# Two changes to a cross-attention loop: where max rows are turned, and which engine reads 8 of 52 max units

## The reference

```python
q = (x @ Wq + bq).reshape(Bq, Tq, 16, 8)        # 1024 queries
k = (ctx @ Wk + bk).reshape(Bk, Tk, 16, 8)      # 6404 keys
v = (ctx @ Wv + bv).reshape(Bk, Tk, 16, 8)
scores = einsum('bqhd,bkhd->bhqk', q, k) / sqrt(8)
attn = softmax(scores, axis=-1)
out = einsum('bhqk,bkhd->bqhd', attn, v).reshape(...) @ wo + bo
```

## Time and profile before

| | us |
|---|---|
| median of 3 runs | 4839.96 (4836.34 to 4844.47) |
| the profiled execution | 4841.48 |
| its span, first to last instruction | 4839.6 |
| busy PE / DVE / ACT / POOL in it | 3934.6 / 3448.6 / 2863.0 / 258.7 |
| busy DVE in max units (L1510) | 2801.6 |
| busy ACT in exponentials (L1497) | 2471.6 |
| mean granted TensorE clock | 0.853 of full |

### The profile page before, as it was taken

The page is one execution under the profiler, slowest core; times in us unless marked ns, Lnnn a source line. Parts: engine busy times, 40 slices in busy tenths (PEclk is TensorE's granted clock), DMA queues, the critical chain, the costliest instruction groups (busy, mean ns, idle before and its releaser), DMA issues. The chain is left out here.

```text
span 4839.6 us, 83868 instructions
## 1 busy us (share of the span) xinstructions
PE 3934.6 (81%) x34310; PEld 1295.2 (27%) x34310; DVE 3448.6 (71%) x3258; ACT 2863.0 (59%) x4073; POOL 258.7 (5%) x183
## 2 busy tenths in 40 slices
PE   6897478988898855888988898479747988898885
PEld 2563222222222212222222222135422222222221
DVE  4332488888888615888888885389848888888871
ACT  1332157777777741677777777335414777777774
POOL 3000000000000010000000000234310000000000
PEclk9556579999998985899999989789957999999998
DMA  2000310111111012110111010100041111011100
GB/s 83 1 0 11 70 22 13 24 24 24 16 21 24 4 37 59 23 24 13 23 24 24 13 24 4 43 19 5 3 81 16 19 24 24 14 23 24 24 2 20
DMA packets 103596, 114.10 MB, mean 24 GB/s; under 512 B 58672, under 2 KB 93712, under 8 KB 98256
## 3 DMA queue, kind: packets, MB, share of 16 engines
q1 hardware_dynamic: 103248, 109.19, 13.3%
HBM read 83.56 MB, written 25.60 MB: 23 GB/s over the span
## 5 line engine op out<-in xcount | busy, mean ns | idle before, releaser
L1510 DVE TENSOR_REDUCE chunk_max<-max_scores 128x2 f32<-128x1024 f32 (+1 forms) x2496 | 2801.6, 1179 | 534.5 <-PE max_scores L1399 408.3
L1497 ACT ACTIVATE probs<-scores 128x512 f32<-128x512 f32 (+1 forms) x3231 | 2471.6, 809 | 907.8 <-PE scores L1425 751.9
L1425 PE MATMUL scores<-queries,key_ring 49*128 49x512 bf16 x4800 | 1288.4, 404 | 244.0 <-ACT probs L1497 129.5
L1452 PE MATMUL values_sum<-probs,values 128*9 128x256 f32 x19584 | 1446.6, 402 | 1.7 <-ACT probs L1497 1.7
L1399 PE MATMUL max_scores<-key_ring,queries 48*128 48x512 bf16 (+1 forms) x4992 | 979.0, 411 | 216.1 <-DVE chunk_max L1510 154.2
L1452 PEld LDWEIGHTS values_sum<-probs,values 128*9 128x9 f32 x19584 | 386.8, 91 | 893.6 <-issue 626.1
L1425 PEld LDWEIGHTS scores<-queries,key_ring 49*128 49x128 bf16 x4800 | 313.1, 95 | 1141.7 <-ACT probs L1497 877.6
L1399 PEld LDWEIGHTS max_scores<-key_ring,queries 48*128 48x128 bf16 x4992 | 249.7, 97 | 645.7 <-DVE chunk_max L1510 555.9
L1057 ACT ACTIVATE probs<-scores 128x512 f32<-128x512 f32 x256 | 138.5, 592 | 106.1 <-PE scores L1009 106.1
L1524 DVE COPY values_sum_s<-values_sum 128x256 f32<-128x256 f32 x48 | 20.1, 418 | 235.0 <-PE values_sum L1452 235.0
L1083 DVE TENSOR_REDUCE chunk_max<-max_scores 128x1024 f32 (+1 forms) x128 | 154.9, 1213 | 23.6 <-PE max_scores L965 23.4
(11 more groups left out here) (176 smaller groups left out, 1944.1 us busy)
## 6 DMA issues: line engine op xcount, KB each, us to landing
key_ring<-k_parts SPq DMA_DIRECT2D x96, 300.2 KB
key_ring<-k_parts SPq DMA_DIRECT2D x96, 200.1 KB
k_parts<-k_part SPq DMA_DIRECT2D x108, 128.0 KB, 2.3
key_ring<-k_parts SPq DMA_DIRECT2D x96, 100.1 KB
o_whole<-values_sum_s SPq DMA_DIRECT2D x48, 128.0 KB, 8.0
queries<-q_parts SPq DMA_DIRECT2D x36, 128.0 KB
context<-in_ctx_t SPq DMA_DIRECT2D x1, 3202.0 KB, 17.5
q_parts<-q_part SPq DMA_DIRECT2D x12, 256.0 KB, 2.8
```

Of the source, the lines that this page charges most:

```text
L1425: return pe.matmul(sc[:, g % 3, :], keys(rows, h, P * t, P * (t + 1)), qb[rows, q], start=True, stop=True)
L1452: mm = pe.matmul(acc[32 * b:32 * b + WV, 0:QBLOCK], vb[rows, h, t, :], pr[rows, slot, QBLOCK * (b % 2):QBLOCK * (b % 2 + 1)], start=(t == ...
L1497: act.activation(pr[:, a % RING:a % RING + b - a, :], sc[:, a % 3:a % 3 + b - a, :], ACT.Exp)\
L1510: dve.tensor_reduce(mx[:, h % 2, c, :, j], mxb[:, u % 2, :, 0:w], AX.X, ALU.max)\
```

## The change

**Max rows.** The DRAM tensor and both waits on it are gone. The 8 columns of `neg_max` are turned by one small matmul against an identity into an ordinary `max_scores` buffer (L1488), VectorE copies the 8 x 128 result to `neg_max_rows` in SBUF (L1634), and SyncE moves two rows from there into `queries` (L1443). This step, the *turn*, is an entry in the row of max units: 45 entries per head now, in place of 52.

**Helped units.** The 8 units of chunks 0 to 7 at j = 0 are made in the ring of the `scores` banks, in place of score slots: five triples per head (numbers 4, 11, 18, 25, 32 of now 39) and one odd operation at the end write max scores there, and ScalarE copies them as bf16 to `helped_scores` (L1601). VectorE folds them: 7 elementwise maxima of 128 x 1024 (L1650), two narrower ones (L1655), a reduction (L1658), in groups of 1, 1, 2, 1 and 2 + 3, each two triples after the copies.

**Numbers.** Exponential operations per head round up to 34 triples; `LEAD` is 6; the opening has 50 max entries, and in it all value projections come after max units, where three had come before the first. Max entries are due after odd operations too. `neg_max` of the next head is made at triple 34, the turn comes at triple 35. SBUF holds two more tiles; the PSUM tiles are the same.

The diff, cut to its core:

```diff
-HEAD_UNITS = 4 * NCHUNK
-NOPS = 2 * (H * HEAD_SLOTS // 3) + (1 if H * HEAD_SLOTS % 3 else 0)
+HELP_CHUNKS = 8
+HELPS = 2 * HELP_CHUNKS
+HELP_AT = [4, 11, 18, 25, 32]
+EXP_TRIPLES = -(-HEAD_SLOTS // 3)
+TRIPLES = EXP_TRIPLES + len(HELP_AT)
+FIRST_OPS = 2 * len(HELP_AT) + 2
+NOPS = 2 * TRIPLES * (H - 1) - 1 + 2 * EXP_TRIPLES - 1
+HEAD_UNITS = 4 * NCHUNK - HELP_CHUNKS
+TURN_AFTER = 2
+NENTRY = H * (HEAD_UNITS + 1)
 RING = 15
 HOLD = 6
-LEAD = 12
+LEAD = 6
 QBLOCK = 256
+HELP_FOLDS = HELP_CHUNKS - 1 + 2
+HEAD_MAX_AT = 34
...
+def exp_slots(h, triple, odd):
+    if h < H - 1 and triple in HELP_AT:
+        return range(0)
+    x = 3 * exps_before(h, triple)
+    return range(x + 2, min(x + 3, HEAD_SLOTS)) if odd else range(x, x + 2)
+def helps_of(h, triple, odd):
+    if h < H - 1 and triple in HELP_AT:
+        i = 1 + 3 * HELP_AT.index(triple)
+        return h + 1, (range(i + 2, i + 3) if odd else range(i, i + 2))
+    if h < H - 2 and triple == TRIPLES - 1 and odd:
+        return h + 2, range(0, 1)
+    return None
...
+def entries_through(n):
+    last = NENTRY if n > op_number(H - 2, HEAD_MAX_AT, 1) else NENTRY - 1
+    return min(last, HEAD_UNITS + LEAD + -(-(HEAD_UNITS + 1) * (n + 1) // (2 * TRIPLES)))
+def max_entry(w):
+    if w < HEAD_UNITS:
+        return 0, w
+    h, v = (w - HEAD_UNITS) // (HEAD_UNITS + 1) + 1, (w - HEAD_UNITS) % (HEAD_UNITS + 1)
+    if h == H or v == TURN_AFTER:
+        return h - 1, None
+    return h, (v if v < TURN_AFTER else v - 1)
+def unit_of(v):
+    tiles = QT // 2 - 1
+    if v < tiles * HELP_CHUNKS:
+        return v // tiles, 1 + v % tiles
+    v -= tiles * HELP_CHUNKS
+    return HELP_CHUNKS + v // 4, v % 4
...
+        nrow = sb("neg_max_rows", [QT, P], BF16)
+        hb = sb("helped_scores", [P, HELPS, CHUNK], BF16)
...
             def max_rows(h):
-                sp.wait_ge(head_max, h + 1)
-                sp.dma_start(nm[h].rearrange("t p -> p t"), nmax[:],
-                             allow_slow_non_contiguous=True).then_inc(max_stored, 16)
-                sp.wait_ge(max_stored, 16 * (h + 1))
+                sp.wait_ge(max_taken, turn_entry(h) + 1)
                 for half in range(2):
                     row = 64 * half + KROWS
                     sp.dma_start(qb[row:row + 1, HALF * h:HALF * (h + 1)].rearrange("o (j p) -> o j p", p=P),
-                                 nm[h:h + 1, 4 * half:4 * (half + 1)]).then_inc(rows_loaded, 16)
+                                 nrow[4 * half:4 * (half + 1), :]).then_inc(rows_loaded, 16)
...
+            def max_entries(lo, hi):
+                for w in range(lo, hi):
+                    h, v = max_entry(w)
+                    if w >= 2:
+                        pe.wait_ge(max_taken, w - 1)
+                    if v is None:
+                        pe.wait_ge(head_max, h + 1)
+                        mm = pe.matmul(mxb[0:QT, w % 2, 0, 0:P], nmax[:], k.ident_b[:], start=True, stop=True)
+                    else:
+                        need_keys(h)
+                        c, j = unit_of(v)
+                        for half in range(2):
+                            mm = max_matmul(mxb[:, w % 2, half, :], h, c, j, half)
+                    mm.then_inc(max_scores, 1)
+            def help_op(at, h, halves_of_units):
+                need_keys(h)
+                for b, i in enumerate(halves_of_units):
+                    mm = max_matmul(sc[:, at + b, :], h, i // 2, 0, i % 2)
+                mm.then_inc(scores_ready, 1)
...
+            def ring_op(n):
+                h, triple, odd = op_place(n)
+                pe.wait_ge(act_done, FIRST_OPS + (n if (h, triple, odd) == (H - 1, 0, 0) else n - 1))
+                help_job = helps_of(h, triple, odd)
+                if help_job is not None:
+                    help_op(2 * odd, *help_job)
+                    return
+                for b, x in enumerate(exp_slots(h, triple, odd)):
+                    if x == 0:
+                        pe.wait_ge(rows_loaded, 32 * (h + 1))
+                    mm = score_slot(h, x, 2 * odd + b)
                 mm.then_inc(scores_ready, 1)
...
-            for c in range(3):
-                value_projection(c)
-            for u in range(HEAD_UNITS + LEAD):
-                max_unit(u)
-                if u % 4 == 3 and u // 4 + 3 < NCHUNK:
-                    value_projection(u // 4 + 3)
-            pe.wait_ge(v_copied, NCHUNK + 1)
+            for w in range(HEAD_UNITS + LEAD):
+                max_entries(w, w + 1)
+                if w < 2 * NCHUNK:
+                    if w % 2 == 1:
+                        value_projection(w // 2)
+                    continue
+                p = w - 2 * NCHUNK
+                if p == 0:
+                    pe.wait_ge(v_copied, NCHUNK + 1)
+                if p < FIRST_OPS:
+                    if p >= 2:
+                        pe.wait_ge(act_done, p if p == FIRST_OPS - 1 else p - 1)
+                    help_op(0 if p % 2 == 1 and p < FIRST_OPS - 1 else 2, *first_help(p))
             pe.wait_ge(v_ones, 1)
             for n in range(NOPS):
-                score_op(n)
-                for u in range(units_through(n - 1) if n else HEAD_UNITS + LEAD, units_through(n)):
-                    max_unit(u)
+                ring_op(n)
+                max_entries(entries_through(n - 1) if n else HEAD_UNITS + LEAD, entries_through(n))
                 for i in range(tiles_by[n - 1] if n else 0, tiles_by[n]):
                     values(i)
...
+            def copy_help(at, h, halves_of_units):
+                a, b = halves_of_units[0], halves_of_units[-1] + 1
+                if a == 0 and h >= 1:
+                    act.wait_ge(folded, h)
+                act.activation(hb[:, a:b, :], sc[:, at:at + b - a, :], ACT.Copy).then_inc(act_done, 1)
...
+            def take_entry(w):
+                h, v = max_entry(w)
+                dve.wait_ge(max_scores, w + 1)
+                if v is None:
+                    if h >= 1:
+                        dve.wait_ge(rows_loaded, 32 * h)
+                    dve.tensor_copy(nrow[:], mxb[0:QT, w % 2, 0, 0:P]).then_inc(max_taken, 1)
+                else:
+                    c, j = unit_of(v)
+                    width = min(CHUNK, M - CHUNK * c)
+                    dve.tensor_reduce(mx[:, h % 2, c, :, j], mxb[:, w % 2, :, 0:width], AX.X, ALU.max)\
+                       .then_inc(max_taken, 1)
+            def fold(h, t):
+                first, last = 3 * t + 1, 3 * t + 4
+                done = HELP_FOLDS * h
+                for unit in range(max(1, first // 2), last // 2):
+                    copied = helps_copied(h, 2 * unit + 1)
+                    dve.wait_ge(act_done, copied)
+                    if unit > 1:
+                        dve.wait_ge(helped, done + unit - 1)
+                    dve.tensor_tensor(hb[:, 0:2, :], hb[:, 0:2, :], hb[:, 2 * unit:2 * unit + 2, :], ALU.max)\
+                       .then_inc(helped, 1)
+                if t == len(HELP_AT) - 1:
+                    for s, width in enumerate((CHUNK // 2, CHUNK // 4)):
+                        dve.wait_ge(helped, done + HELP_CHUNKS - 1 + s)
+                        dve.tensor_tensor(hb[:, 0:2, 0:width], hb[:, 0:2, 0:width], hb[:, 0:2, width:2 * width], ALU.max)\
+                           .then_inc(helped, 1)
+                    dve.wait_ge(helped, done + HELP_FOLDS)
+                    dve.tensor_reduce(mx[:, h % 2, 0, :, 0], hb[:, 0:2, 0:CHUNK // 4], AX.X, ALU.max).then_inc(folded, 1)
+            def head_maximum(h, entries):
+                dve.wait_ge(max_taken, entries)
+                dve.wait_ge(folded, h + 1)
...
+            for w in range(HEAD_UNITS + LEAD):
+                take_entry(w)
+                t = (w - 2 * NCHUNK - 4) // 2
+                if w % 2 == 0 and 0 <= t < len(HELP_AT):
+                    fold(0, t)
+                if w == HEAD_UNITS - 1:
+                    head_maximum(0, w + 1)
+            units_done = 1
+            for n in range(NOPS):
+                for w in range(entries_through(n - 1) if n else HEAD_UNITS + LEAD, entries_through(n)):
+                    take_entry(w)
+                    if max_entry(w)[1] == HEAD_UNITS - 1:
+                        ready, units_done = w + 1, units_done + 1
+                h, triple, odd = op_place(n)
+                if h < H - 1 and odd and triple - 2 in HELP_AT:
+                    t = HELP_AT.index(triple - 2)
+                    fold(h + 1, t)
+                if h < H - 1 and odd and triple == HEAD_MAX_AT:
+                    assert units_done == h + 2
+                    head_maximum(h + 1, ready)
+                if n and tiles_by[n] // NTILE > tiles_by[n - 1] // NTILE:
+                    take_values(tiles_by[n - 1] // NTILE)
```

155 lines of the change are left out of this document (80 added, 75 removed).

## The result

Measured together, the kernel before took 4838.15 us (median of 4, 4828.01 to 4844.47) and the changed one 4967.61 us (median of 4, 4964.05 to 4970.75): ratio 1.0269 (1.0250 to 1.0289). The forecast was 4927 us. The profiled execution took 4966.19 us, its span is 4964.4 us, its mean granted clock 0.852 (before: 0.853).

What follows compares the result with a forecast made beforehand. VectorE was taken to bound the middle of a head. With the change, 66.4 + 3.3 + 2.0 = 71.7 us per head against 69.2, so 4841.5 + 112 - 27 = 4927 us; range 4780 to 5045.

Steps and rivals of the forecast that it cites:

- ring, TensorE not waiting: ScalarE and TensorE set a head's beat over 39 triples: 66.4 us per head if TensorE never waits for VectorE.
- wait at the turn: TensorE waits at the turn for neg_max behind VectorE's folds: 3.3 us lost per head, 4.8 at the high end.
- half clock behind it: After the turn's wait, TensorE at its lower clock for 5 us at 0.4: 2.0 us per head, bounds 0 and 4.
- head: One head of the changed kernel: 71.7 us against 69.2, + 2.5 us, 45 times: + 112 us.
- opening: First max unit to first score of a layer: 76.2 us instead of 85.2, saving 9 us three times.
- keeps its upper clock: Rival: TensorE's clock stays up in the 10 us after triple 35; head middle 69.3 us, 4819 us total; chance 0.25.
- Folds: VectorE's elementwise maxima over helped scores: 0.69 us each at the low end, which the forecast took, 1.22 at the high.
- slow folds: Rival: folds run at one element per cycle, wait 4.8 us, 73.8 us per head, 5033 us total; chance 0.11.
- Part one: Max rows without the DRAM round trip: store, joint stall and row waits go, worth some 7 us per head alone.
- The stall isn't the store's: Rival: the joint stall of three engines has another cause, 3.9 us per head stay, 5100 us total; chance 0.06.
- Half clock in more places: Rival: triples without values tiles after helped ones lose clock too, + 3.5 us per head, 75.2 us, 5085 us; chance 0.08.
- part two: Helped units in the ring of ScalarE and TensorE: 39 triples instead of 33 2/3, costing more than Part one's some 7 us per head.

Runs made afterwards that it cites:

- e4_fill_wait: Changed kernel with 48 small matmuls on TensorE right ahead of its wait at the turn, result not the reference's: 4751.06 us, ratio 0.9686.
- e1_rows_only: Kernel before with only the max rows turned by a matmul and moved inside SBUF; no helped units, old ring and opening: 4609.37 us, ratio 0.9392.
- e5_wide_store: e1_rows_only plus an unread store of neg_max to DRAM in 128 pieces of 16 bytes: 4606.65 us, ratio 0.9488.
- e6_rows_and_opening: e1_rows_only with no value projection ahead of the opening's max units and one after every second unit: 4568.08 us, ratio 0.9410.
- e11_wide_store_and_opening: Kernel before with neg_max stored in 16-byte pieces, row loads gathering 2-byte elements, and the opening order of e6_rows_and_opening: 4570.57 us, ratio 0.9317.
- e8_help_five: Changed kernel with 5 helped units per head instead of 8, neg_max at triple 32, turn three units behind the last max unit: 4568.40 us, ratio 0.9411.
- e2_rows_and_store: e1_rows_only plus the old element-wise store of neg_max to DRAM, whose result nobody reads: 4867.86 us, ratio 0.9927.
- e3_turn_later: Changed kernel with helped triples one earlier, neg_max at triple 33 and the turn one entry later: 4692.41 us, ratio 0.9559.

## Why the prediction was right and where it was not

**Right:** slower, inside the range, and the mechanism: the change takes the pace of a head from VectorE, puts the turn's wait of 3.2 us (forecast 3.3) into every head, and the clock falls with it. That the 4927 us are within 0.8% of the result is luck: two errors offset each other. 45 heads cost 206 us instead of 112, three openings gave 74 instead of 27, the last heads 9 instead of 0.

Step by step, in us per head:

| term | forecast | measured |
|---|---|---|
| ring, TensorE not waiting | 66.4 | 65.6 = 68.8 (`e4_fill_wait`, clock 1.00) - 3.2 |
| wait at the turn | 3.3 | 3.2 |
| half clock behind it | 5 x 0.4 = 2.0 | 73.6 - 68.8 = 4.8, or 14.2 x 0.34 |
| head | 71.7 | 73.6 |
| opening | 76.2 | 60.2 |

- **The half clock's length is the term that was mis-sized.** I took 5 us "behind it" with no row for this length; the earlier trace rows showed 9 us at half clock in one place and about 17 in a head. The measured stretches are 6.8, 20.5 and 23.9 us, and the term, 4.8 us, lies outside its bounds of 0 and 4. Its price of 0.4 us per us was a little high: 4.8 / 14.2 = 0.34, nearer to the 0.35 of the earlier trace rows. In `e4_fill_wait` the term vanishes with TensorE's idle time alone, which the rival "keeps its upper clock" priced at 69.3 us for a head: it measured 68.8. The rival was priced right, but didn't happen by itself.
- **The ring was right within 1 us,** in its kinds of triple (1.51, 1.57 and 1.79 us as forecast, 1.94 or 2.01 for the 2.01 forecast) and in their count: by the code's table 9 triples of a head have a max unit between odd score and two values tiles, 8 between odd score and one. On ScalarE's timeline seven triples go from 1230.90 to 1242.52:

```profile
1230.90 4.60 ACT L1619 ACTIVATE probs<-scores 128x1024 f32<-128x1024 f32 x6 [0.28 <-PE scores L1523]
1235.92 3.02 ACT L1619 ACTIVATE probs<-scores 128x1024 f32<-128x1024 f32 x4 [0.43 <-PE scores L1523]
1239.22 1.51 ACT L1619 ACTIVATE probs<-scores 128x1024 f32<-128x1024 f32 x2 [0.27 <-PE scores L1523]
1240.73 1.51 ACT L1601 ACTIVATE helped_scores<-scores 128x1024 bf16<-128x1024 f32 x2
1242.52 1.02 ACT L1619 ACTIVATE probs<-scores 128x1024 f32<-128x1024 f32 x1 [0.28 <-PE scores L1523]
```

  Of its 11.62 us, 7 x 1.51 = 10.57 are ScalarE's own work and 1.05 are idle (0.43, 0.27 and 0.28 ahead of even operations and the rest inside the three triples of 4.60 us). The forecast's terms give 1.2 for the same seven. A head isn't 39 times a seventh of this stretch (that would be 64.7 us): at its ends stand triples of 1.9 to 2.1 us (`e4_fill_wait`).
- **Folds:** 685 ns, the low end, so the slow folds fall away. VectorE: DVE Perf Modes, "The perf-mode tier table", of the Trainium skill gives elementwise operations on two 16-bit tensors in SBUF twice the rate of f32; the trace agrees, 1024 elements in 685 ns against 1224 ns for the same shape in f32.
- **Part one** was right in cause and too large in size: "some 7 us per head" measured 4.4 (`e1_rows_only`). I priced the stall of the earlier trace rows, 4 us, in every head. The earlier trace rows had the average: VectorE's remote idle time is 105.8 us, 2.2 us in each of 48 heads. One instance of a wait was taken for its mean. And the half clock doesn't go with the stall altogether: of about 10 us per head before, 4.6 stay. The receipt of the last write, which the prediction mentions beside the store's 13.3 us, doesn't explain them: the wide store of `e5_wide_store` writes the same 2 KB to DRAM and lands in 1.4 us.
- **Opening:** the sum's term 13 x 0.99 us failed. The gap behind a projection in the earlier trace rows was taken as the price of a projection. It belongs to that order, with three projections ahead and the rest after every fourth unit: in the new order the whole stretch with projections has 0.96 us of such gaps. The order alone is worth 8 us (`e6_rows_and_opening`) or 7 (`e11_wide_store_and_opening`). It also raises the clock: in the first half of the opening it is 0.50 in `e1_rows_only` and 0.91 in `e6_rows_and_opening`. What of the 8 us is the clock's and what the order's own was not separated.
- **The stall isn't the store's:** no. It goes with the store (`e1_rows_only`) and comes back with it (`e2_rows_and_store`).
- **Half clock in more places:** no. The triples without values tiles keep the clock at 1.00 (the window of seven triples above, and `e8_help_five` without any half clock in its heads).

**Where part two's loss comes from.** Part one alone takes 4609 us, the changed kernel 4959, in sets where before took 4907 and 4905. Of these 350 us, 267 go with the wait at the turn (4959 to 4692 in `e3_turn_later`, which also moves folds and helped triples by one), and what is left of helping eight units is 83. The forecast's "part two costs more than that" is right, but most of the cost is the place of the turn in TensorE's order, not the copies and folds.

**Open:** what decides whether 7, 20 or 24 us at half clock follow the same wait of 3.2 us; why part one alone has stretches of 6.8 us behind idle times of 0.7 us; why the last heads are 3 us shorter (54.3 or 54.4 us in every kernel with the new ring); why before differs by 1.4% between sets of runs; and why some stores bring no stall and others one of up to 5.9 us.

## What to carry to other kernels

A wait of TensorE is priced by the clock behind it as well as by its length. Take the length of the half clock from all such stretches that the trace has, not from a guess: before had stretches of up to 20.5 us in its heads and some 10 us of it per head, the forecast put 5, and the changed kernel has stretches of up to 23.9. Before a transposing store is replaced by matmuls, buffers and waits, try to write DRAM in 16-byte pieces and let the load do the transposing. Price a stall by the mean over all places where it can stand, not by one instance. And price a step in the middle of an order by what it costs in the new order: a gap behind an instruction isn't the instruction's price.
